# The sum of the rotation's two products on GpSimd in place of VectorE, from the fourth pair of token tiles on

## The reference

```python
x = x + attn(layernorm(x))       # 16 heads of 8 channels, rotary positions, causal window of 64 keys
x = x + ffn(layernorm(x))        # a shared expert, and 4 of 32 routed experts per token, with a capacity

def _apply_rope(q, k):
    ...
    q = q * cos + _rotate_half(q) * sin
    k = k * cos + _rotate_half(k) * sin
```

## Time and profile before

| | us |
|---|---|
| median of 3 runs | 600.62 |
| the three runs | 596.67, 600.62, 604.53 |
| the profiled execution, its own time | 604.68 |
| span of the profiled execution | 602.5 |
| busy in it: TensorE / VectorE / GpSimd / ScalarE | 513.2 / 424.7 / 343.0 / 323.1 |

### The profile page before, as it was taken

One profiled execution on the slowest core, in us unless ns is written; L12 is line 12 of the kernel. 1 busy time (PEld: TensorE's weight loads), 2 busy tenths in 40 slices (PEclk: granted clock), 3 DMA queues, 4 the chain that ended last, 5 costly groups with the idle time before them and its releaser, 6 DMA issues.

```text
span 602.5 us, 20827 instructions
## 1 busy us (share of the span) xinstructions
PE 513.2 (85%) x7427; PEld 423.3 (70%) x7427; DVE 424.7 (70%) x1297; ACT 323.1 (54%) x832; POOL 343.0 (57%) x362
## 2 busy tenths in 40 slices
PE   3558997989988798887669889999989999999756
PEld 2336665766666566665545589999989999998544
DVE  5666799779999899966676366756666676664264
ACT  3336775767777677655546225455446555454200
POOL 8520113276666566655777507777777777777600
PEclk9659998989999999977899979999999999999977
DMA  7889998887877665520000134543534554541198
GB/s 254 234 234 249 250 248 235 225 268 212 240 231 208 210 209 151 137 66 25 21 12 10 36 99 140 150 123 108 164 119 140 171 155 149 170 118 49 24 394 292
DMA packets 79417, 98.33 MB, mean 163 GB/s; under 512 B 12097, under 2 KB 59999, under 8 KB 79216
## 3 DMA queue, kind: packets, MB, share of 16 engines
q1 hardware_dynamic: 65280, 82.92, 47.2%
q0 software_dynamic: 9216, 12.02, 6.4%
q10 hardware_dynamic: 4848, 2.40, 1.4%
HBM read 50.00 MB, written 54.30 MB: 173 GB/s over the span
## 4 chain that ended last, share of the span: by engine, by line
PE 38%; DVE 6%; DMA 5%; issue 4%; POOL 3%; ACT 2%; SPq 0%; POOLq 0%; DVEq 0%; ACTq 0%
PE banks L1115 18%; PE banks L1141 12%; DMA rload<-pair_results 3%; PE banks L1126 3%; POOL expert_slots L490 2%; DVE mx L1239 1%; PE banks L932 1%; DMA pair_results<-yout,yidx 1%; PE banks L1050 1%; POOL pair_results L618 1%; PE banks L1167 0%; DMA xg<-expert_slots 0%; SPq L440 0%; PE banks L874 0%; ACT yout L805 0%
## 5 line engine op out<-in xcount | busy, mean ns | idle before, releaser
L618 POOL DMA_INDIRECT pair_results<-yout,yidx x160 | 159.3, 996 | 67.0 <-issue 38.1
L490 POOL DMA_INDIRECT expert_slots<-xfe,sidx x128 | 127.8, 998 | 89.7 <-issue 38.9
L1115 PE MATMUL banks<-xgT_parts,wgu_parts 128*128 128x320 f32 x768 | 131.3, 320 | 1.9 <-DVE hact L1506 1.7
L1115 PEld LDWEIGHTS banks<-xgT_parts,wgu_parts 128*128 128x128 f32 x768 | 113.9, 190 | 4.6 <-DVE hact L1506 2.3
L1239 DVE TENSOR_REDUCE mx<-banks 128x8 f32<-128x1024 f32 x64 | 78.0, 1219 | 21.0 <-PE banks L882 21.0
L1506 DVE TENSOR_TENSOR hact<-hact,banks 128x320 f32<-128x320 f32 x128 | 56.6, 482 | 43.0 <-ACT hact L786 42.1
L805 ACT ACTIVATE yout<-banks,ypair 128x128 f32<-128x128 f32 x160 | 44.8, 372 | 76.2 <-PE banks L1141 73.8
L655 ACT ACTIVATE pt<-banks 128x512 f32<-128x512 f32 x128 | 69.3, 593 | 27.9 <-PE banks L913 26.6
L1141 PE MATMUL banks<-wdn,hact 128*128 128x128 f32 x640 | 76.6, 275 | 1.1 <-DVE hact L1506 1.1
L1141 PEld LDWEIGHTS banks<-wdn,hact 128*128 128x128 f32 x640 | 75.0, 192 | 1.3 <-issue 1.3
L786 ACT ACTIVATE hact<-banks 128x320 f32<-128x320 f32 x128 | 53.5, 452 | 33.1 <-PE banks L1115 31.4
(11 more groups left out here) (154 smaller groups left out, 945.5 us busy)
## 6 DMA issues: line engine op xcount, KB each, us to landing
expert_slots<-xg SPq DMA_DIRECT2D x32, 325.0 KB, 4.8
xg<-expert_slots SPq DMA_DIRECT2D x32, 325.0 KB
pair_results<-zero SPq DMA_DIRECT2D x32, 256.0 KB
rload<-pair_results SPq DMA_DIRECT2D x16, 512.0 KB, 8.9
kS<-rotated_keys SPq DMA_DIRECT2D x32, 240.0 KB
qS<-rotated_queries SPq DMA_DIRECT2D x32, 192.0 KB
wgu<-in_L_ffn_wg_dram SPq DMA_DIRECT2D x32, 128.0 KB
wgu<-in_L_ffn_wu_dram SPq DMA_DIRECT2D x32, 128.0 KB
```

Of the source, the lines that this page charges most:

```text
L490: g.indirect_dma_start(out=slots_d, out_offset=bass.IndirectOffsetOnAxis(ap=sidx[:, m % NB, j, k:k + 1], axis=0), in_=xfe[:, m % NB, j, k, ...
L618: g.indirect_dma_start(out=pairs_d, out_offset=bass.IndirectOffsetOnAxis(ap=yidx[:, c, j:j + 1], axis=0), in_=yout[:, c, j, :], in_offset= ...
L1115: last = mm(bank[2 + 2 * w + h][:, 0:CH], wgu_parts[:, e.b, wp, w, h * P:(h + 1) * P], xgT_parts[:, e.b, xp, ch * CH:(ch + 1) * CH], start ...
```

## The change

From `f = 3` on VectorE leaves the sum out of `rotate()`; GpSimd makes it. Where pair `y` exists (`f` from 7 to 15) it stands after `dispatch(y, 1, 1)`, in the place of the wait for `rope_sum`; where it doesn't (`f` from 3 to 6) it is the first instruction of GpSimd's step. GpSimd waits for both products, and for the readers of the previous `rr` (ScalarE's rounding and VectorE's `rest()`); VectorE's products wait for the previous sum, so that they don't overwrite its inputs.

```diff
+    ROPE_POOL = 3
...
+                def rotated():
+                    pool.wait_ge(S.rope_c, f + 1)
+                    pool.wait_ge(S.rope_s, f + 1)
+                    wait(pool, S.split_hi, f)
+                    wait(pool, S.split_rest, f)
+                    g.tensor_tensor(rr[:, :, :], ta[:, :, :], tb[:, :, :], ALU.add).then_inc(S.rope_sum, 1)
...
                     dispatch(y, 1, 1)
                     if f is not None:
-                        behind(S.rope_sum, f + 1)
+                        rotated()
                     elif s is not None:
                         behind(S.exp_done, NU * s + 4)
                     dispatch(y, 1, 2)
                     paced(6)
                     dispatch(y, 1, 3)
+                if y is None and f is not None and f >= ROPE_POOL:
+                    rotated()
                 if z is not None:
                     ready(z)
...
                         dve.wait_ge(S.proj_done, 2 * f + 2 - q)
+                        wait(dve, S.rope_sum, f)
                         v.tensor_tensor(t[:, :, :], bk[:, :].rearrange("p (c t) -> p c t", c=2),
...
-                    dve.wait_ge(S.rope_c, f + 1)
-                    dve.wait_ge(S.rope_s, f + 1)
-                    wait(dve, S.split_hi, f)
-                    v.tensor_tensor(rr[:, :, :], ta[:, :, :], tb[:, :, :], ALU.add).then_inc(S.rope_sum, 1)
+                    if f < ROPE_POOL:
+                        dve.wait_ge(S.rope_c, f + 1)
+                        dve.wait_ge(S.rope_s, f + 1)
+                        wait(dve, S.split_hi, f)
+                        v.tensor_tensor(rr[:, :, :], ta[:, :, :], tb[:, :, :], ALU.add).then_inc(S.rope_sum, 1)
```

## The result

The changed kernel is slower by a little more than one per cent: ratio to the kernel before 1.0121, 95% interval 1.007 to 1.0173, from six runs of each (medians 611.24 and 601.42 us). On the median of before the ratio makes 7.3 us (4 to 10).

A forecast was written before the change was run, and what follows sets the result against it. Transfers bind until 122 us, then VectorE in pairs 8 to 15. Terms 0 (early sums) + 0.9 (pair 8) + 2.2 (pairs 9 to 15) = 3.1 us, giving 603.7 us on the median of 600.62; range 598 to 609, own range 602 to 607.

The forecast's parts named there:

- the forecast's mechanism: Pairs 8 to 15: VectorE's `rest()` waits for GpSimd's later sum and ScalarE's rounding; 3.1 us slower in all.
- its own sign: VectorE's `rest()`, line 1285: the prediction called itself wrong if this line doesn't wait; it expected about 1 us of waiting.
- the five early sums: Pairs 3 to 7, before 122 us: waits for transfers swallow any change on VectorE, so they count nothing.
- pair 8's lateness from the fills: Pair 8, with GpSimd still behind from the slot fills: `rest()` starts 0.87 us later, 0.9 in the forecast's total.
- the late sum: GpSimd's sum behind `dispatch(y, 1, 1)`: `rest()` starts 0.32 us later per step, 2.2 us over pairs 9 to 15.
- D: Length of the 128x512 sum on GpSimd, estimated at 1.05 us; a step changes by D - 0.73, the whole by 8 D - 5.3.
- So it should not meet: VectorE's small product in `gates()`, 0.5 us ahead of GpSimd's sum: claimed not to collide with it on the shared SBUF port.
- the port rival: Small product of `gates()` waits behind GpSimd's whole sum: `rest()` 0.93 to 1.1 late, eight steps, about 8 us; 12 in 100.
- the sum's removal: VectorE's sum in `rotate()`: leaving it out frees 0.71 us a step, 5.7 us over eight steps with nothing else changed.
- the short-sum rival: GpSimd's sum takes only 0.514 us: seven steps win 0.22 each, pair 8 loses 0.33, -1.2 us in all; 10 in 100.
- The 2.2 us ahead of `second_norm()`: Slack between the end of GpSimd's power and VectorE's `second_norm()`, claimed to cover GpSimd coming about a microsecond later.
- TensorE's cover of 0.86 us: TensorE's spare time before needing VectorE's marks; ScalarE, 0.64 later than VectorE, was to leave 0.2 of it.

The follow-up runs named there:

- e3: Changed kernel with only the sums of pairs 8 to 15 on GpSimd, those of pairs 3 to 7 back on VectorE; ratio to the kernel before 1.0144.
- e4: Changed kernel with only the sums of pairs 3 to 7 on GpSimd, those from pair 8 on back on VectorE; ratio to the kernel before 1.0022.
- e1: Changed kernel with GpSimd's sum also waiting until the small product of `gates()` is done; ratio to the kernel before 1.006.
- e2: Changed kernel with the sum placed ahead of the second dispatch on GpSimd; ratio to the kernel before 1.0123.
- e10: Kernel before with the sum made nowhere, rounding and `rest()` reading the product `ta` instead; ratio to the kernel before 0.9985.
- e6: Changed kernel with `gates()` ahead of the products and `rest()` moved behind `add_attention()` and `second_stats()` on VectorE; ratio to the kernel before 0.9977.
- e9: Changed kernel with the product of `gates()` written as two `tensor_scalar` instructions with a per-partition scalar; ratio to the kernel before 1.0075.

## Why the prediction was right and wrong

**The size was less than half.** Forecast 3.1 us, measured 7.3 (4 to 10): within 2%, slower as the sum said, but by the mechanism of a rival that had 12 in 100, not by the forecast's. The forecast's own range, 602 to 607 us, was missed by about a microsecond (600.62 x 1.0121 is 607.9); that the time is within 598 to 609 is owed to the room that was left for the rival, and for the forecast's mechanism it is luck. By its own sign the prediction was wrong: line 1285, now 1297, doesn't wait.

**Right: the place.** Only pairs 8 to 15 count, as far as e3 and e4 can tell. The stretch up to 122 us swallowed the five early sums, with the blocks of pairs 6 and 7, as the waits of the earlier trace rows had it; pair 8's lateness from the fills varied with the execution and wasn't needed.

**Right: the late sum, as a formula.** The step changes by D - 0.73, and e1, where nothing else stands in the way, gives it to 0.01 us. The term mis-sized is D: 1.05 us by the write's pace, 1.28 measured (1266 to 1288 ns over the 13):

```profile
L535 POOL TENSOR_TENSOR rr<-ta,tb 128x512 f32<-128x512 f32 x13 | 16.6, 1280 | 34.7 <-DVE ta L1279 34.5
```

The estimate of 1.12 from the Trainium skill's figure was nearer and low as well. With 1.28 the forecast's own sum would have been 8 x 1.28 - 5.3 = 4.9 us.

**Wrong: "So it should not meet".** This is the step that failed. The price of the port rival was right (0.93 to 1.1 late in eight steps; 0.94 and eight), its condition was judged by the wrong clock. The prediction put the product 0.5 us ahead of the sum's start and called it safe; in the trace it does start 0.53 ahead (151.46 against 151.99) and is shut out nevertheless. What counts is not when the sum's span begins. The sum's hold on VectorE began by 151.46 at the latest, and two cases say what it needs. In e1 its waits are met only when the product is done; it begins at the same place behind the dispatch and shuts nothing out. In e3's pair 8 its waits were met at 130.99, ahead of the product, but the dispatch right ahead of it had not begun; nothing was shut out either. In pair 9 both were so (`ta` ended at 151.36, the dispatch began at 151.00). So the hold goes by the later of the two; the second of them rests on one pair. e2 agrees: with no dispatch ahead, span and block coincide, 1.26 and 1.27 us. The rule that the prediction cited (whoever starts first keeps the port) holds only if "starts" is read so. How the sum can hold the port while a dispatch still runs ahead of it is argued, not shown: the Trainium skill (GPSIMD Engine Reference, instruction dispatch) says that each of GpSimd's eight cores goes on to the next instruction as soon as it has done its share of the last, so those that have nothing to do in a dispatch could begin on the sum.

**Wrong: what the relief is worth.** The prediction read from 15.23 of 16 us that "each microsecond that VectorE loses or wins there moves the attention stage's end", and priced the sum's removal at 0.71 us a step. Removed without anything in return (e10) it is worth 0.09: for 4.94 us of each step VectorE's next maxima hang on TensorE's scores, and the sum was in that stretch. It didn't spoil the forecast, since the loss was counted from the old schedule. But the gain that the short-sum rival counted on (0.22 us a step) was not to be had beyond 0.1.

**Covers.** The 2.2 us ahead of `second_norm()` held: in pairs 8 to 15 of the changed kernel VectorE never waits for GpSimd's power. TensorE's cover of 0.86 us wasn't used up either, as VectorE was late too: TensorE still waits there for VectorE's marks in the changed kernel (up to 1.0 us). ScalarE's lateness mattered only where VectorE's waits were covered: in e6 TensorE waits for its exponentials.

## What to carry to other kernels

Before work is moved to GpSimd, look at the VectorE instructions that work on SBUF alone and come after the moment at which GpSimd's waits are met, however small they are, and also while a dispatch right ahead on GpSimd still runs: an 8-element product took 1.85 us here instead of 0.17 because it stood behind such a moment, and one more wait on the sum made the step shorter. An engine that is busy for 95% of a step isn't thereby the only bound (without 0.71 us of its work the step lost 0.09): leave the work out altogether for one run, and see what its removal is worth, before looking for another place for it. Where a move must be late, have work that needs neither its result nor the shared port ready to fill the gap, as e6 does.

## What the runs showed of the hardware

- A 128x512 fp32 sum of two SBUF tensors takes 1.28 us on GpSimd and 0.69 on VectorE.
- A GpSimd sum can keep a VectorE instruction out ahead of its recorded start, while the indirect DMA right ahead of it still runs: 1.85 us of block for a sum of 1.28. It didn't where its waits weren't met yet (e1: 0.17 us), nor where that DMA hadn't begun (e3, pair 8: 0.17).
- Shut out were `tensor_tensor` with two SBUF tensors and `tensor_scalar` with a per-partition scalar (e9: 1.84 us), and not a sum of SBUF and PSUM (e6: 0.42 us) nor maxima out of PSUM (e1: 1.22, from 162.72, beside a sum from 163.16).
- The other way round, a dispatch beside VectorE's sum took 1.37 us; without that sum, in the same place of the changed kernel, 0.96.
